# Four residual layers on one core: zero products in two prologue waits, an earlier second product, and one x split moved behind an eviction

## What is computed

```
x = x + conv(x, L0_weight)  + c @ L0_c_weight.T + bias      # 9 taps, 4 groups of 32 channels
x = x + agg1 @ x + b1                                       # 128 x 128 matrix of its own for each sample
x = x + agg2 @ x + b2
x = x + conv(x, L3_weight)  + c @ L3_c_weight.T + bias

h    = gelu(gelu(c @ W0 + b0) @ W1 + b1)                    # c: the condition, 32 x 128
att  = softmax(h @ W2 + b2)                                 # 8 weights for each sample
agg  = sum over k of att[k] * weight[k];   b = att @ bias_k
```

## Time and profile before

| | us |
|---|---|
| median of 3 runs | 675.3 (673.67 to 676.19) |
| the profiled execution, its time | 675.1 |
| its span in the trace | 673.3 |
| TensorE busy | 657.8 (98%) |
| VectorE busy | 487.5 (72%) |
| ScalarE busy | 262.3 (39%) |
| GpSimd busy | 247.4 (37%) |
| mean share of the 16 DMA engines in the core's queue 1 | 80.7% |

### The profile page before, as it was taken

The page is one execution under the profiler, slowest core; times in us unless marked ns, Lnnn a source line. Parts: engine busy times, 40 slices in busy tenths (PEclk is TensorE's granted clock), DMA queues, the critical chain, the costliest instruction groups (busy, mean ns, idle before and its releaser), DMA issues.

```text
span 673.3 us, 24658 instructions
## 1 busy us (share of the span) xinstructions
PE 657.8 (98%) x11222; PEld 589.9 (88%) x11222; DVE 487.5 (72%) x940; ACT 262.3 (39%) x329; POOL 247.4 (37%) x91
## 2 busy tenths in 40 slices
PE   9999999999999999999999999999999999999994
PEld 6789899988888888888888888888888888888884
DVE  5798768677667767766877776787777677677646
ACT  5352433333443343343334244334324433433435
POOL 6022543323443342444243344424244433434220
PEclk9699999999999999999999999999999999999998
DMA  7417888898888899888889888889988888977636
GB/s 230 135 47 158 198 194 194 149 219 157 195 197 193 172 179 186 181 192 194 189 154 214 164 192 195 193 174 173 195 176 198 196 193 165 188 159 156 135 90 157
DMA packets 50181, 118.24 MB, mean 176 GB/s; under 512 B 5541, under 2 KB 26074, under 8 KB 42330
## 3 DMA queue, kind: packets, MB, share of 16 engines
q1 hardware_dynamic: 49586, 116.95, 80.7%
q10 hardware_dynamic: 360, 0.69, 0.5%
q0 software_dynamic: 192, 0.02, 0.0%
HBM read 35.33 MB, written 33.55 MB: 102 GB/s over the span
## 4 chain that ended last, share of the span: by engine, by line
PE 93%; DVE 2%; DMA 2%; ACT 1%; issue 1%; SPq 0%; ACTq 0%; POOL 0%; DVEq 0%; POOLq 0%
PE ps L826 76%; PE ps L896 13%; DMA mix_w<-prod 1%; PE ps L988 1%; PE ps L883 1%; DMA out_planes<-out_taps 1%; PE ps L945 1%; ACT out_sb L541 1%; DVE y_lo L628 0%; DVE x_lo L614 0%; SPq L330 0%; DVE prod_sum L675 0%; DVE acc L667 0%; DVE mat L667 0%; DVE out_taps L648 0%
## 5 line engine op out<-in xcount | busy, mean ns | idle before, releaser
L400 POOL COPY out_sb<-out_planes 128x2048 f32<-128x2048 f32 x30 | 119.3, 3978 | 276.5 <-DMA out_planes<-out_taps 276.5
L471 ACT ACTIVATE y_hi<-ps,bias_tab 128x512 fp32r<-128x512 f32 x128 | 77.5, 689 | 192.4 <-PE ps L826 192.4
L394 POOL COPY x_planes<-x_in 128x2048 f32<-128x2048 f32 x29 | 112.8, 3889 | 96.0 <-DVE x_lo L614 96.0
L638 DVE SCALAR_TENSOR_TENSOR z_lo<-ps,bias_tab,z_hi 128x1024 fp32r<-128x1024 f32 x62 | 76.7, 1279 | 68.4 <-ACT z_hi L481 68.3
L628 DVE SCALAR_TENSOR_TENSOR y_lo<-ps,bias_tab,y_hi 128x512 fp32r<-128x512 f32 x128 | 87.2, 744 | 45.3 <-ACT y_hi L471 45.3
L826 PE MATMUL ps<-z_hi,taps_lo 32*128 32x512 f32 x1488 | 99.8, 398 | 0.8 <-issue 0.8
L826 PE MATMUL ps<-x_hi,taps_hi 32*128 32x512 f32 x1536 | 97.7, 391 | 1.0 <-DVE out_taps L648 1.0
L826 PE MATMUL ps<-x_lo,taps_hi 32*128 32x512 f32 x1536 | 98.2, 397 | 0.0
L826 PE MATMUL ps<-x_hi,taps_lo 32*128 32x512 f32 x1536 | 97.3, 391 | 0.0
L826 PE MATMUL ps<-z_hi,taps_hi 32*128 32x512 f32 x1488 | 93.0, 391 | 0.5 <-ACT prod_sum L549 0.5
L489 ACT ACTIVATE out_taps<-ps,bias_tab 128x512 f32<-128x512 f32 x62 | 39.3, 685 | 137.3 <-PE ps L826 137.3
(11 more groups left out here) (119 smaller groups left out, 566.3 us busy)
## 6 DMA issues: line engine op xcount, KB each, us to landing
x_in<-in_x SPq DMA_DIRECT2D x31, 1024.0 KB, 11.0
out_planes<-out_taps SPq DMA_DIRECT2D x122, 256.0 KB, 7.6
out<-out_sb SPq DMA_DIRECT2D x30, 1024.0 KB, 4.2
mix_w<-prod SPq DMA_DIRECT2D x128, 128.0 KB, 4.6
x_in<-in_x SPq DMA_DIRECT2D x2, 512.0 KB, 5.2
out<-x_planes SPq DMA_DIRECT2D x8, 128.0 KB, 2.2
out_taps<-in_L_cond_weight SPq DMA_DIRECT2D x1, 512.0 KB, 5.2
mix_w<-in_L_cond_weight SPq DMA_DIRECT2D x1, 512.0 KB, 6.4
```

What stands on the lines that cost most here:

```text
L394: pool.tensor_copy(x_planes[:, :, :], planes(x_in[t.par(d)], slice(0, S))).then_inc(x_planed, 1)
L400: pool.tensor_copy(out_sb[t.par(d)][:, :].rearrange("c (s p) -> c p s", p=PH), out_planes[:, :, :])\
L471: act.activation(y_hi[:, g, :], ps[:, bank(t, 0) + g, :], ACT.Identity, bias=bias_tab[:, b, g:g + 1]).then_inc(y_hi_done, 1)
L638: dve.scalar_tensor_tensor(out=z_home(t, 0)[1][:, 2 * h:2 * h + 2, 1:S + 1], in0=ps[:, k:k + 2, :], scalar=bias_tab[:, b, 2 * G:BIAS], in1 ...
```

## The change

In three places:

1. `keep_busy` gets an argument for the PSUM banks that it writes. Three calls are added in the prologue, all writing bank 4: 3 zero products before the first product of the two matrices, 4 before the first five `mixed_bias`, 2 before the last five. Ahead of the first stands a wait for `att_tab_done`, since bank 4 held that table.
2. `product(zero, 1)`, the product for the second sample, stands four turns before the end of the second sample's conv0, not behind it.
3. In VectorE's `one(t)` for t = 2, x_lo of the next sample stands behind the eviction of sample 1, not ahead of it.

```diff
--- before.py
+++ after.py
@@ -703,13 +703,15 @@
                     low_y(t)
                 if t.has(1):
                     split_product(t, 1)
-                if t.has(1):
+                if t.has(1) and not t.at(2):
                     low_x(t, 1)
                 if t.at(N - 1):
                     low_z(t)
                     turn_upper()
                 else:
                     evac_out(t, -1)
+                    if t.at(2):
+                        low_x(t, 1)
                     low_z(t)
 
             def turn_upper():
@@ -982,10 +984,10 @@
                     last = pe.matmul(o, ones[0:1, 0:N], key_b[l], start=False, stop=True)
                 last.then_inc(logits_psum, 1)
 
-            def keep_busy(n):
+            def keep_busy(n, banks=range(G)):
 
                 for i in range(n):
-                    pe.matmul(ps[:, i % G, :], y_hi[:, 0, 0:C], y_hi[:, 0, :], start=True, stop=True)
+                    pe.matmul(ps[:, banks[i % len(banks)], :], y_hi[:, 0, 0:C], y_hi[:, 0, :], start=True, stop=True)
 
             zero, first = Step(0, 0), Step(0, 1)
             pe.wait_ge(zeros_done, 1)
@@ -1030,11 +1032,15 @@
             conv_biases()
             conv0(zero, range(16, 19))
             pe.wait_ge(agg_done, 1)
+            pe.wait_ge(att_tab_done, 1)
+            keep_busy(3, (4,))
             product(zero, 0)
             conv0(zero, range(19, 21))
+            keep_busy(4, (4,))
             for k in range(MIXED // 2):
                 mixed_bias(k)
             conv0(zero, range(21, 2 * SHIFTS))
+            keep_busy(2, (4,))
             for k in range(MIXED // 2, MIXED):
                 mixed_bias(k)
             conv0(zero, range(2 * SHIFTS, TURNS))
@@ -1043,8 +1049,9 @@
             pe.wait_ge(prod_summed, 1)
             conv0(first, range(14))
             mix(zero)
-            conv0(first, range(14, TURNS))
+            conv0(first, range(14, TURNS - 4))
             product(zero, 1)
+            conv0(first, range(TURNS - 4, TURNS))
             for t in ALL[1:2 * LOOP[0]]:
                 one(t)
             with pe.Fori(LOOP[0], LOOP[1]) as half:
```

## The result

| | before | changed |
|---|---|---|
| median of 7 runs each, us | 675.30 (673.11 to 676.19) | 671.73 (670.57 to 672.03) |
| profiled execution, us | 675.1 | 671.78 |
| its span | 673.3 | 670.0 |

A forecast was written before the change was run, and what follows sets the result against it. TensorE, busy 98% of a 673.3 us span, was taken as the bound, so only its waits or low clock could give time; 4.1 + 0.5 + 1.0 = 5.6 us off 675.1 gave 669.5 us, range 668.6 to 672.2.

The forecast's parts named there:

- the first and the third rival: Sample 0's conv0: clock falls later, up to 2.3 us back (12%); parts 2 and 3 only move waits, 671.0 us (4%).
- Part 1: Prologue: nine zero products keep TensorE's clock up, 5.0 us gained less 0.94 for the zeros, net 4.1 us.
- Part 2: Sample 1's conv0: the product four turns earlier hides ScalarE's copy behind 16 matmuls, gaining 0.5 us.
- Part 3: VectorE at sample 2: eviction ahead of the x split removes TensorE's wait for it, gaining 1.0 us.
- fourth rival: Slower (2%): moved x split delays copy and load, eviction wait returns sample after sample; ten waits give 680.8 us.
- second rival: Prologue: zeros don't hold the clock, which falls at 23.2 us for as long as before; 674.8 us (9%).
- the rule on idle gaps: Prologue: by it the two short waits didn't lower the clock, filling them wouldn't hold it; time 674.8 us.
- The price of the low clock: TensorE in the prologue, about 23.2 to 33.4 us: 5.0 us together, between 4.7 and 5.2, before the zeros' cost.

The follow-up runs named there:

- zeros_alone: The kernel before with the nine zero products alone, without the earlier second product and the moved x split; 671.67 us, 0.9956 of before.
- changed_again: The changed kernel itself, timed again on one chip with three other kernels; 671.91 us, 0.9964 of before.
- two_inputs: Changed kernel with the product's high half written by a two-input maximum in place of VectorE's one-input copy; 671.45 us, 0.9953 of before.
- seven_zeros: Changed kernel without the last two zero products; 670.45 us, 0.9948 of before.
- split_behind_all: Changed kernel with VectorE evicting sample t-1 before splitting the next sample's x in every sample; 669.02 us, 0.9923 of before.
- weave_behind_split: Changed kernel with GpSimd's weave, from sample 3 on, waiting until VectorE has split the product of sample t+1; 672.09 us, 0.9962 of before.
- split_all_seven: Changed kernel with the eviction ahead of the x split in every sample and without the last two zero products; 668.69 us, 0.9926 of before.
- split_all_weave_loop: Changed kernel with the eviction first in every sample and GpSimd's weave behind the product's split for samples 3 to 27; 669.78 us, 0.9937 of before.

## Why the prediction was right, and where it was wrong

The time, 671.73, lies in the range of 668.6 to 672.2 and the sign is right. In part that is luck: it lies above the 668.8 to 670.5 that the forecast itself allowed, and the upper part of the range was there for the first and the third rival, a clock that falls later and waits that move to the next place. What took the time is neither as described. (By the sum's own ends the lower one should be 669.25, not 668.8: 675.1 less 4.3, 0.52 and 1.03.) Step by step:

- **Part 1, the clock: right, size 3.8 for 4.1.** The clock stayed up, the zeros took 0.28 us each (the last two from 25.41 to the next row's 25.98), 44 matmuls of the last third 2.81 us. The missing 0.3 lies ahead of it: VectorE's matrices were done 0.3 us later in this execution (product at 21.29, not 20.98), because a load of x landed later and ScalarE's work ahead of them with it. That is a difference between executions, not of the change: with the same zeros the first mix started at 33.47 in zeros_alone and at 33.46 in changed_again, 4.15 us ahead of before. y_lo of sample 0 began at 31.06, not 30.7.
- **Part 2: 0.57 for 0.5. Part 3: 1.02 for 1.0.** Both by the mechanism given.
- **The step that failed** is the first paragraph's: "What TensorE gains in the first 80 us is therefore kept to the end, unless it meets another engine's work: the others have room in each sample." It did meet another engine's work. The room was read from where VectorE was idle, and it was there; but one of its instructions can be stretched from 0.23 to over 3 us by GpSimd's copy, and the trace of before showed that already, with 18 CASTs of 0.47 to 1.04 us among those of 0.23. I had not asked what ended them. 2.1 of the 5.5 us went again, part of it in this wait and part in gaps put down to issue, 1.0 of it at sample 28; the medians show 3.6 of the 5.6 forecast.
- **The fourth rival** had the right kind (a wait for the eviction comes back later) with the wrong cause and size: not the x split or its load, but the weave; one to three waits between samples 3 and 7, 1.1 to 2.5 us together in the four traces of the changed order with zeros and all three parts (changed, changed_again, two_inputs, seven_zeros), not ten.
- **The second rival** falls, and with it, for this case, what the prediction drew from the rule on idle gaps of the Trainium skill (TensorE: Matmul & The Clock Gate, Why this matters for your kernels): without zeros the clock fell in each of the four kernels traced, behind waits of 0.8 to 1.0 us like those of the earlier trace rows, and with the waits filled it fell in none of ten.
- **The first and third rival**: no trace with seven or nine zeros shows a fall before the tail. No run with them has a mean clock under 0.994, except in the two kernels with the weave's wait, where it goes down to 0.992; where in those runs the clock was low, their traces don't say. The third comes near in effect: the gain of parts 2 and 3 is gone by sample 7, though not by a wait at the next place.
- The chance of 85% for over 0.5% was too sure: the measured gain is 0.5%, and its interval lies on both sides.
- The price of the low clock was read from one execution in which it lasted 10 us. In 29 runs of before on one chip the mean granted clock goes from 0.995 in the fastest (671.33 us) to 0.988 in the slowest (676.00). On that chip the slower runs are those with the lower clock. The changed kernel's 12 runs beside them stay at 0.994 to 0.996 and within 2.2 us. That the clock is not all of the spread is seen in seven_zeros, 3.8 us wide at 0.995 to 0.996.

## What to carry to other kernels

A lead gained in the prologue lasts only if every engine keeps its distance to the others: ask which instructions now fall together that did not before, and look in the trace for one whose duration varies from sample to sample, since its long values say what it will cost when they become the rule. Where VectorE and GpSimd read SBUF at the same time and can't be kept apart, put what TensorE waits for ahead of what has room; that gave 2.7 us here by medians from different chips, and 3.2 on one chip with two zeros fewer, while separating the two by a wait gave nothing. Before calling a gap the cause of a late end, ask whether the chain that ended last runs through it. And a price read from one execution (here of the low clock) can be near one end of a spread over runs.

## What the runs showed of the hardware

**TensorE's larger gaps without a releaser end shortly behind a transfer of instructions.** The waits put these gaps down to "issue". The profile names the kind of queues 8 and 14 "instruction", and not whose they are; that queue 8 feeds TensorE is inferred from the times below. The queues of the changed kernel's trace, first from 140 to 580 us, then from 580 to 662:

```profile
q1 hardware_dynamic: 31966, 81.27, 88.6%
q14 instruction: 10, 0.08, 0.1%
```

```profile
q8 instruction: 12, 0.20, 1.2%
```

Between 140 and 580 us, in the loop, there are no packets of queue 8; in the unrolled samples behind it there are 12, and TensorE has a gap behind two of them. The last packet and the end of TensorE's last gap, in us:

| kernel | last fetch | gap ends | gap |
|---|---|---|---|
| before | 660.7 to 662.4 | 663.87 | 0.59 |
| changed | 657.4 to 659.1 | 660.52 | 0.75 |
| zeros_alone | 656.6 to 658.3 | 659.76 | 0.80 |
| split_behind_all | 655.5 to 657.2 | 658.72 | 0.89 |
| weave_behind_split | 657.3 to 659.0 | 660.32 | 2.44 |

In each, TensorE goes on 1.3 to 1.5 us after the fetch has ended; in split_all_seven it is 1.9 us, for a gap of 1.51. The gap of 0.74 us at 586, the first sample behind the loop, is of the same kind: fetch from 583.6 to 584.6, on at 586.11; the sample took 20.82 us there against 19.83 before, which is the 1.0 us that the lead lost between samples 27 and 28. In the five kernels of the table the last gap is not on the chain that ended last, which goes by the last relay and ScalarE; in split_all_seven and split_all_weave_loop it is. All this was read in the traces and not tried by an edit, so that a late fetch makes the gap is likely and not shown.

**The wait of VectorE for GpSimd** lasts to the end of GpSimd's instruction, and it holds for a copy and for a maximum of two inputs alike: 1.54 and 1.55 us in the mean, 0.23 for the copy where they are kept apart. When the CAST comes just ahead of the weave, the next instruction waits in its place: in split_all_weave_loop the subtraction behind the CAST, two inputs in SBUF, took 3.67 us at 384.94 in place of 0.29, beside a weave from 384.76 to 388.64. And it goes both ways: in weave_behind_split the weave at 88.01 started while VectorE's x split ran (87.80 to 90.09) and took 5.83 us in place of 3.9.
